# Third mixture of a decoder kernel: eight blocks of rows made on chip by products with slot tables

## The reference

```python
x_flat = x.reshape(s * b, h)                       # 1024 x 128
probs = jax.nn.softmax(x_flat @ gate_w.T / TEMPERATURE, axis=-1)
topk_probs, topk_idx = jax.lax.top_k(probs, TOPK)  # TOPK = 2
hidden = jax.nn.relu(jnp.einsum('th,ehf->tef', x_flat, w1) + b1[None])   # f = 512
all_out = jnp.einsum('tef,efh->teh', hidden, w2) + b2[None]
gathered = jnp.take_along_axis(all_out, topk_idx[:, :, None], axis=1)
y_flat = jnp.sum(gathered * topk_probs[:, :, None], axis=1)
```

## Time and profile before

| | us |
|---|---|
| median of 3 runs | 1390.26 (1382.43 to 1390.34) |
| the profiled execution, whole time | 1389.44 |
| its span, from the first to the last instruction | 1387.6 |
| PE busy | 1152.1 |
| DVE busy | 889.7 |
| POOL busy | 272.7 |

### The profile page before, as it was taken

How to read it: one execution, slowest core, us unless ns; L and a number is a source line. 1 busy time by engine, 2 the same in 40 slices (tenths; PEclk the granted TensorE clock), 3 DMA queues, 4 the chain that set the end, 5 groups by cost and what they waited for, 6 DMA issues and landing times.

```text
span 1387.6 us, 26416 instructions
## 1 busy us (share of the span) xinstructions
PE 1152.1 (83%) x9412; PEld 712.4 (51%) x9412; DVE 889.7 (64%) x2335; ACT 711.6 (51%) x1456; POOL 272.7 (20%) x558
## 2 busy tenths in 40 slices
PE   4878997894887499668999999999944968989994
PEld 2333333892343498455666666666634833333332
DVE  5758985445667354877766666677740176777866
ACT  3665883231733123325666665776712535646674
POOL 2522221461010274100000000000024404212220
PEclk9798998996897699889999999999976978989998
DMA  7421248554311496200000000011034734211200
GB/s 179 104 73 42 67 129 344 196 174 144 79 52 61 160 309 216 97 0 1 1 1 1 1 1 1 9 46 47 24 110 133 263 121 103 64 48 48 54 8 16
DMA packets 91362, 122.45 MB, mean 88 GB/s; under 512 B 11073, under 2 KB 69134, under 8 KB 90254
## 3 DMA queue, kind: packets, MB, share of 16 engines
q1 hardware_dynamic: 87010, 112.11, 26.1%
q0 software_dynamic: 4224, 8.66, 1.9%
HBM read 89.73 MB, written 30.02 MB: 86 GB/s over the span
## 4 chain that ended last, share of the span: by engine, by line
PE 64%; DVE 14%; DMA 6%; issue 5%; ACT 5%; POOL 3%; SPq 3%; DVEq 0%; ACTq 0%; POOLq 0%
PE ps L2717 7%; PE ps L2724 7%; PE ps L1170 6%; PE ps L2732 6%; PE ps L1865 4%; PE ps L920 4%; PE ps L1878 3%; PE ps L929 3%; PE ps L2806 2%; PE ps L1867 2%; PE ps L2813 2%; PE ps L1082 2%; PE ps L1205 2%; POOL scr_x L2120 2%; PE ps L970 2%
## 5 line engine op out<-in xcount | busy, mean ns | idle before, releaser
L1170 PE MATMUL ps<-probs,vaug 128*32 128x256 f32 (+1 forms) x1792 | 144.9, 398 | 12.0 <-ACT probs L1134 7.5
L2924 DVE CUSTOM_DVE_ANT_0 wring<-ps,probs 128x768 f32<-128x768 f32 x128 | 122.5, 957 | 46.2 <-PE ps L2717 45.6
L2883 ACT COPY qs<-ps 128x768 f32<-128x768 f32 x128 | 102.3, 800 | 90.3 <-PE ps L2724 90.3
L1125 ACT ACTIVATE probs<-ps 128x512 f32<-128x512 f32 x192 | 104.2, 595 | 64.3 <-PE ps L970 64.1
L273 POOL TENSOR_TENSOR rstd<-veps,mhalf 128x4 f32<-128x4 f32 (+2 forms) x28 | 26.5, 948 | 538.2 <-DVE veps L241 503.0
L1002 DVE TENSOR_REDUCE mx<-ps 128x2 f32<-128x1024 f32 (+1 forms) x96 | 115.5, 1220 | 20.7 <-PE ps L920 19.9
L1129 ACT ACTIVATE probs<-ps 128x512 f32<-128x512 f32 x192 | 104.8, 595 | 40.9 <-PE ps L1082 39.8
L2864 ACT ACTIVATE wring<-wring,r 128x768 f32<-128x768 f32 x128 | 120.8, 944 | 3.9 <-DVE r L2927 3.9
L2724 PE MATMUL ps<-ident,wring 128*128 128x128 f32 x768 | 110.2, 280 | 3.2 <-DVE wring L2968 3.2
L2724 PEld LDWEIGHTS ps<-ident,wring 128*128 128x128 f32 x768 | 83.4, 140 | 41.9 <-issue 35.3
L2717 PE MATMUL ps<-probs 64*128 64x512 f32 (+1 forms) x512 | 100.5, 511 | 1.1 <-DVE r L2924 1.1
(11 more groups left out here) (383 smaller groups left out, 2405.3 us busy)
## 6 DMA issues: line engine op xcount, KB each, us to landing
wring<-in_L_ffn_w SPq DMA_DIRECT2D x21, 768.0 KB, 5.9
wring<-in_L_ffn_w SPq DMA_DIRECT2D x19, 514.0 KB, 4.9
ks<-in_L_ffn_w SPq DMA_DIRECT2D x8, 768.0 KB, 16.5
qs<-in_L_ffn_w SPq DMA_DIRECT2D x6, 768.0 KB, 11.3
probs<-scr_x SPq DMA_DIRECT2D x14, 256.0 KB, 4.0
qs<-scr_q SPq DMA_DIRECT2D x18, 192.0 KB
qs<-scr_qx SPq DMA_DIRECT2D x16, 192.0 KB
probs<-in_L_ffn_w SPq DMA_DIRECT2D x4, 768.0 KB
```

Of the source, the lines that this page charges most:

```text
L1125: act.activation(probs[:, s % 2, 2 * c + r, kt0 * S:(kt0 + 2) * S], bank(self.banks(3, k)[r]), ACT.Exp).then_inc(p_exp.sem, 1)
L1170: ins = pe.matmul(ps[32 * j:32 * j + 32, self.av_bank(s), q0:S], vaug[:, s % 2, kt, j, :], probs[:, s % 2, j, at:at + S - q0], start=(kt = ...
L2883: act.copy(self.pT[:, g % 2, j, :, k * P:(k + 1) * P], self.buffer("turn", i, 0, KV).rearrange("p (t n) -> p t n", n=P)).then_inc(self.out ...
L2924: dve.tensor_tensor_reduce(self.sc[:, s, :], src, self.maskb[:, u // (2 * PR), :], 1.0, -3.0e38, ALU.add, ALU.max, self.top[:, s:s + 1]).t ...
```

## The change

- Rows of blocks 0 to 7 (groups 0 and 1) are made on chip. For each group g and token tile t DVE makes a slot table of 128 x 512 (`hot_vector`): at row p, column j a one where either slot of token p is column j of the group. It takes two instructions, a comparison of the column numbers (`self.numbers`, in `gated`) with the first slot, and a second comparison added to it. PE multiplies `h[:, t, :]` with the table and sums over the eight tiles in one bank (`permute_tensor`), which gives the group's rows already turned; ACT copies them to `xbT` as before. There are 16 tables in a ring of four, in the memory of `v`. Twelve are made behind the slots in `place_vector`, the last four behind the results of blocks 0 and 1. PE does the first eight products before block 0 and two more before each of blocks 1 to 4.
- The 16 scatters stay. The loads of groups 0 and 1 go, and group g + 2 is loaded behind the weights of block 4g + 3. The wait for all 16 scatters stays behind the weights of block 3.
- The map and the shares move behind the products: DVE does them in pieces at blocks 4 to 8 and PE behind the up matmuls of block 7. The column sums of the last part's weights (`weights_vector`) move from block 6 to block 10.
- `constant_rows` moves from ahead of SP's loop to behind the weights of block 12.

```diff
@@ -1577,13 +1577,13 @@
     r_exp = counter("r_exp", [1] * 3)
     sorted_out = counter("sorted_out", [NT, 0, 2 * NT], 16)
     h_spill = counter("h_spill", [pair_loads[8], 4, 0], 16)
-    hot = counter("hot", [m["choices"] for m in MOES])
+    hot = counter("hot", [1, 2, 2 * NT + 2])
     map_mm = counter("map_mm", [1] * 3)
     mapped = counter("mapped", [2] * 3)
-    x_in = [counter(f"x_in{i}", [len(range(i, groups[0], 2)), 2, len(range(i, groups[2], 2))], 16) for i in range(2)]
+    x_in = [counter(f"x_in{i}", [len(range(i, groups[0], 2)), 2, len(range(i, groups[2], 2)) - 1], 16) for i in range(2)]
     x_rows = [counter(f"x_rows{i}", [0, sum(min(2, blocks[1] - 2 * g) for g in range(i, groups[1], 4)), 0],
                       16) for i in range(4)]
-    x_tp = counter("x_tp", groups)
+    x_tp = counter("x_tp", [groups[0], groups[1], groups[2] - 2])
...
@@ -1704,7 +1708,8 @@
             m, n = self.m, self.group(g)
             rows = slice(g * self.gb * P, (g * self.gb + n) * P)
             if g >= self.held:
-                sp.wait_ge(x_tp.sem, x_tp.at(m, g - self.held + 1))
+                if g - self.held >= self.turned_in:
+                    sp.wait_ge(x_tp.sem, x_tp.at(m, g - self.held - self.turned_in + 1))
...
@@ -1726,8 +1731,6 @@
                     for k in range(2):
                         sp.dma_start(scr_h[1 + k * T:1 + (k + 1) * T, :].rearrange("(t p) d -> p t d", p=P)[:, at, :],
                                      h[:, at, :]).then_inc(h_spill.sem, 16)
-            if self.relu:
-                constant_rows(sp)
...
@@ -1741,9 +1744,10 @@
                 if self.sorted:
                     if b == self.early:
                         sp.wait_ge(sorted_out.sem, sorted_out.at(m, self.choices * NT))
-                        self.x_sync(sp, 0)
-                    if b == self.early or b > self.early and b % self.gb == 0 and b // self.gb + 1 < self.ng:
-                        self.x_sync(sp, b // self.gb + 1)
+                    if b % self.gb == self.early and b // self.gb + self.turned_in < self.ng:
+                        self.x_sync(sp, b // self.gb + self.turned_in)
+                    if b == 12:
+                        constant_rows(sp)
...
+            if not self.turned_in:
+                self.map_tensor(pe)
+            for b in range(self.nb):
+                g = b // self.gb
+                if b == 0 and self.turned_in:
+                    self.permute_tensor(pe, range(NT))
+                elif b == 0:
+                    self.turn_tensor(pe, 0)
+                if b % self.gb == self.gb // 2 and g + 1 < self.ng and g + 1 >= self.turned_in:
+                    self.turn_tensor(pe, g + 1)
+                if 0 < b <= self.gb and self.turned_in:
+                    self.permute_tensor(pe, range(NT + 2 * b - 2, NT + 2 * b))
+                self.up_tensor(pe, b)
+                if b:
+                    self.down_tensor(pe, b - 1)
+                if self.turned_in and b == 7:
+                    self.map_tensor(pe)
...
+        def permute_tensor(self, pe, steps):
+
+            m = self.m
+            for i in steps:
+                g, t = divmod(i, NT)
+                pe.wait_ge(hot.sem, hot.at(m, i + 1))
+                ins = pe.matmul(bank(6 + g % 2), h[:, t, :], self.slot_hot[:, i % 4, :], start=(t == 0), stop=(t == NT - 1))
+                ins.then_inc(perm_mm.sem, 1)
+
+        def hot_vector(self, dve, i):
+
+            m = self.m
+            g, t = divmod(i, NT)
+            out, slot = self.slot_hot[:, i % 4, :], slotf[:, g, :, t:t + 1]
+            if i >= 4:
+                dve.wait_ge(perm_mm.sem, perm_mm.at(m, i - 3))
+            link(dve, dchain, dve.tensor_scalar(out, self.numbers, slot[:, 0, :], None, ALU.is_equal))
+            dve.scalar_tensor_tensor(out=out, in0=self.numbers, scalar=slot[:, 1, :], in1=out, op0=ALU.is_equal,
+                                     op1=ALU.add).then_inc(hot.sem, 1)
+
+        def numbers_vector(self, dve):
+
+            for k in range(4):
+                ins = dve.tensor_scalar(self.numbers[:, k * P:(k + 1) * P], down[:, 34:162], float(k * P), None, ALU.add)
+            link(dve, dchain, ins)
 
...
@@ -1881,7 +1927,10 @@
 
         def turn_scalar(self, act, g):
             m, n, first = self.m, self.group(g), self.at(g * self.gb)
-            act.wait_ge(x_tp.sem, x_tp.at(m, g + 1))
+            if g < self.turned_in:
+                act.wait_ge(perm_mm.sem, perm_mm.at(m, (g + 1) * NT))
+            else:
+                act.wait_ge(x_tp.sem, x_tp.at(m, g - self.turned_in + 1))
...
@@ -1908,7 +1957,9 @@
                 k, g = self.sh + b, b // self.gb
                 if b == 0:
                     self.turn_scalar(act, 0)
-                if b % self.gb == self.gb // 2 and g + 1 < self.ng:
+                if self.turned_in and b == self.gb:
+                    self.turn_scalar(act, 1)
+                if b % self.gb == self.gb // 2 and g + 1 < self.ng and (g or not self.turned_in):
                     self.turn_scalar(act, g + 1)
...
@@ -2002,10 +2053,18 @@
             if self.sorted:
                 dve.tensor_scalar(place[:, 0:self.choices * NT], slotf[:, 0, 0:self.choices, :].rearrange("p k t -> p (k t)"),
                                   -1.0, None, ALU.add).then_inc(placed.sem, 1)
-            if self.choices == 2:
+            if self.turned_in:
+                link(dve, dchain, dve.tensor_scalar(slotf[:, 1, :, :], slotf[:, 0, :, :], -512.0, None, ALU.add))
+                for i in range(NT + 4):
+                    self.hot_vector(dve, i)
+            elif self.choices == 2:
                 self.map_vector(dve)
-            if self.choices == 2:
-
+                self.shares_vector(dve)
+
...
@@ -2083,12 +2163,23 @@
                     if y >= RING:
                         dve.wait_ge(y_spill[y % 4].sem, y_spill[y % 4].at(m, y // 4))
                     dve.tensor_copy(yblk[:, self.at(y), :], bank(4 + y % 2, 0, P)).then_inc(y_sb.sem, 1)
+                if self.turned_in and b in (1, 2):
+                    self.hot_vector(dve, NT + 2 + 2 * b)
+                    self.hot_vector(dve, NT + 3 + 2 * b)
+                if self.turned_in and b == 4:
+                    self.map_rows_vector(dve)
+                if self.turned_in and b in (5, 6):
+                    self.map_hot_vector(dve, b - 5)
+                if self.turned_in and b == 7:
+                    self.map_found_vector(dve)
+                if self.turned_in and b == 8:
+                    self.shares_vector(dve)
                 if m == 1 and 2 <= b < 2 + 2 * CTX_STEPS:
                     others[7].context_vector(dve, *divmod(b - 2, CTX_STEPS))
-                if m == 2 and b == 6:
+                if m == 2 and b == 10:
                     others[11].weights_vector(dve)
```

More of the change, by code:

```diff
@@ L1629, in __init__ @@
             self.gb, self.held = GB[m], RING // GB[m]
+            self.turned_in = 2 if self.relu else 0
+            self.hots = self.turned_in * NT
             at = 4608 if self.shared else 5632
             hots = tmp[:, at:at + 512 * self.choices].bitcast(BF16)
+            self.slot_hot = v[:, :, :].rearrange("p (i k) d -> p i (k d)", k=4)
+            self.numbers = gated[:, 0, :]
             self.row_hot = hots.rearrange("p (i j) -> p i j", j=P)
@@ L1790, in tensor, with map_tensor @@
                 self.shared_down_tensor(pe)
+            if not self.turned_in:
[15 more added lines that the diff above has]
+                    self.map_tensor(pe)
+            self.down_tensor(pe, self.nb - 1)
+            if self.relu:
+                pe.wait_ge(y_sb.sem, y_sb.at(m, self.nb))
+                for t in range(NT):
+                    ins = pe.transpose(bank(0 + t // 4, t % 4 * P, t % 4 * P + P)[0:8, :], comb[:, t, 0:8], ident[:, :])
+                ins.then_inc(perm_mm.sem, 1)
+                pe.wait_ge(combT_sb.sem, combT_sb.at(m, 1))
+                for t in range(NT):
+                    ins = pe.matmul(bank(2 + t // 4, t % 4 * P, t % 4 * P + P), combT[:, t * P:(t + 1) * P],
+                                    b2r[:, :], start=True, stop=True)
+                ins.then_inc(perm_mm.sem, 1)
+        def map_tensor(self, pe):
+            m = self.m
+            if self.turned_in:
+                pe.wait_ge(x_T.sem, x_T.at(m, self.turned_in))
             for k in range(self.choices):
-                pe.wait_ge(hot.sem, hot.at(m, k + 1))
+                pe.wait_ge(hot.sem, hot.at(m, self.hots + k + 1))
                 for i in range(k * NT, (k + 1) * NT):
@@ L1850, in turn_tensor @@
                 pe.wait_ge(x_T.sem, x_T.at(m, g))
+            if self.turned_in and g == 3:
+                pe.wait_ge(mapped.sem, mapped.at(m, 1))
             for k in range(n):
@@ L2024, in map_vector, with map_slots, map_rows_vector @@
         def map_vector(self, dve):
-            m, n = self.m, self.choices * NT
+            self.map_rows_vector(dve)
+            for k in range(self.choices):
```

(22 more changed lines are left out.)

36 lines of the change are left out of this document (12 added, 24 removed).

## The result

The changed kernel takes 1394.66 us (median of 10 runs, 1390.83 to 1398.01); the kernel before, on the same chip in the same rounds, 1387.88 (1382.43 to 1392.05). The ratio is 1.0045, 95% interval 1.0025 to 1.0065: 6.8 us slower. That is within 1% and inside the range, but the forecast was 1.4 us faster, so its direction is wrong. The profiled execution took 1392.43, span 1390.6, 3.0 more than before's; the stage that the change touches, read from slots to last copy, accounts for 4.8 more, less 1.5 for slots that are ready earlier (1029.78 against 1031.29). Those profiles are one execution each, and the two are closer together than the medians are.

What follows compares the result with a forecast made beforehand. The prediction took the kernel as mostly bound by PE (83% busy). Block 4 at 1062.8 plus 45.0 us put the last copy at 1107.8 instead of 1109.2, 1.4 us earlier: forecast 1388, range 1377 to 1397.

Steps and rivals of the forecast that it cites:

- What bounds the kernel: Whole kernel: mostly bound by PE, busy 83% of the span; PE stands still around the third mixture's 16 scatters.
- part 1: Products up to block 4: block 0 starts at about 1043 instead of 1059.1, a gain of 16 us on the page.
- Part 2: Block 4's weights, still behind the scatters: block 4 starts at 1060.0 against 1067.81, so 8 of 16 us are left.
- Part 3: Scatters beside DVE's tables: each waits for the DVE instruction in progress, the last lands 2.8 us later; block 4 at 1062.8.
- Part 4: From block 4 to the last copy: 45.0 us instead of 41.4, from several small terms.
- The constant rows: Term from block 4 on: four issues ahead of block 13's weights and 288 KB in a full queue, 1.2 us.
- Results wait for the map: Term from block 4 on: result scatters start only behind the map, block 8's copy waits for the fifth; 0.8 us.
- The clock: Term from block 4 on: PE, after standing still, may begin block 4 at clock 0.50; 1.5 us, between 0 and 2.7.
- A: Rival: scatters aren't slowed and small terms hide behind each other, stage ends 7 us earlier, 1382; chance 0.28.
- The lock: Rival B: DVE's tables hold the scatters' port longer, 6 us in all, stage ends 7 us later, 1396; chance 0.13.
- C: Rival: the whole 16 us of the products come out, needing block 4's weights by 1056; 1373; chance 0.05.
- L: Theory added after the measurement, not in the prediction: from block 4 on the weight loads' own rate sets the pace.

Runs made afterwards that it cites:

- e9: Kernel before, with eight useless DVE instructions of 1.25 us added beside the scatters, four with two inputs, then four with one; 1392.85 us in one execution.
- e2: Kernel before, with only the constant rows moved behind the weights of block 12; 1400.16 us, ratio 1.0100 to before.
- e11: Changed kernel with the map at block 4 instead of block 7, constant rows still late; 1396.05 us, ratio 1.0044 to before.
- e12: e1 with the map at block 4 instead of block 7; 1381.96 us, ratio 0.9956 to before.
- e8: e1 plus four loads, together 288 KB over 128 partitions, behind the weights of block 12; 1388.59 us, ratio 0.9995 to before.
- e1: Changed kernel with the constant rows back ahead of SP's loop; 1389.48 us, ratio 1.0010 to before.
- e5: e1 with block 4's weights issued ahead of the wait for the scatters, some row loads one block later; 1386.16 us, ratio 0.9984 to before.
- e6: e5 with the map at block 4 instead of block 7; 1377.52 us, ratio 0.9922 to before.
- e3: Changed kernel with the late constant rows sent one to a transfer, ten transfers instead of four, each written as 16 runs; 1397.85 us, ratio 1.0077 to before.

## Why the prediction was wrong, step by step

**What bounds the kernel, and part 1: right.** Block 0 started 11.8 us after the slots (11.7 forecast), PE would have been ready for block 4 when ACT's second copy ended, at 1055.00 + 0.59 = 1055.59, that is 25.8 us after the slots (24.7 forecast), and this was hidden, as said, by the wait for block 4's weights.

**Part 2: right, term by term.** From the last landing (1052.77) to the issue 1.17 us (1.25 forecast), landing 4.45 (4.4), a wait of 3.46 us on PE (4). Block 4 started 28.65 us after the slots, where the same steps without a slowed scatter give 28.7.

**Part 3: wrong, and in the kernel's favour.** The step "one has to stand still until the DVE instruction in progress ends ... 2.8 us" didn't occur: the 16 scatters' starts spread over 20.0 us, 20.1 in before. That DVE can hold a scatter is so (e9), but two rows didn't say which of DVE's instructions do, and I took the two engines' instructions to meet at random. They fell into step: in the second view of after each scatter starts 0.04 or 0.05 us behind the start of a two-input instruction, and the pair of DVE's instructions grew by some 0.08 us, from 0.48 + 0.75 to 0.54 + 0.77, until a table took as long as a scatter's period, 1.26. The tables paid, by nearly nothing, and the scatters as a whole nothing.

**Part 4: here the direction was lost.** 54.1 us instead of 45.0, in two of its terms.

- "The constant rows ... 1.2, between 0 and 2.4." The term was worked out from bytes at the mean rate of the queue. Measured: 5.2 us in the changed kernel, 12.0 in the kernel before (e2), 14.1 with the map early (e11 against e12). What failed is the choice of the row: bytes at a mean rate price a transfer like e8's, of short runs over all partitions (it cost nothing), and not one of a few long rows into a few partitions. Before, the rows ran in a quiet time: in the stretches there, from 1022 to 1031, the queues moved no more than 95 GB/s at a share of 0.43. These stretches stand in no row above, and alone they wouldn't have told the reason, since little else was moved then.
- "Results wait for the map ... 0.8, between 0 and 3." The mechanism was right, the copy of block 8 waiting for the scatter of block 4's results; the size was wrong. In e1, without the rows, PE stood still for 5.49 us against the 2 to 3 that I took:

```profile
1070.51 0.18 DVE L2131 TENSOR_TENSOR probs<-probs 128x23 int32<-128x23 int32 x1
...
1072.15 1.06 PE L1924 MATMUL ps<-wring,probs 128*128 128x128 f32 x8
...
1081.82 2.05 PE L1924 MATMUL ps<-wring,probs 128*128 128x128 f32 x8 [5.49 <-DVE probs L2165]
```

The map is there at 1070.69. The fifth scatter lands at 1076.49 + 4.77 = 1081.26, 10.6 us behind it, where I had 7.3: its landing takes 4.77 in a full queue instead of the 2.2 of a quiet one. And the copy of block 8 is due at 1073.21, 2.5 us behind the map, where I had 4 to 5. I also let the stall hide behind a wait for weights, which it doesn't. The late map is worth 7.5 us (e1 against e12).

"The clock ... 1.5" was for a start of block 4 at 0.50. In the changed kernel it didn't come: those eight up matmuls took 1.16 us and the next group 1.06, at a granted clock of 1.00. In e1 they did start low (2.08 us). The fall that the changed kernel had came behind the stall, with 2.04 us for the next down matmuls; it is part of what both terms measured. The map's 16 matmuls took 0.56 us (0.6 forecast); the weights in hand (-0.5) are too small for these runs to hold against anything.

**The rivals.** A (1382) was right on the scatters and wrong on "the small terms hide behind each other". The lock (1396) met the time within 2 us by a mechanism that didn't occur. It had also taken the map's wait at its upper end, 3; a time that fits is no evidence for its reasons. C needed block 4's weights earlier: e5 made exactly that, with the rows ahead, and won only 3.3 us over e1; the copy's stall was still there. With the map early too (e6) the kernel reaches 1377.52.

**Still open:** how the row transfers slow the others. That their place in the queue costs this much is shown (e1, e2, e11 against e12), and that it isn't their bytes (e8). Whether it is the few partitions, the packets of 32 KB or where they are read from isn't: e3 was to tell and left the packets whole. Rows over 128 partitions in long packets, or short packets into the same eight partitions, would tell. L was only argued.

## What to carry to other kernels

Price a transfer by its shape as well as by its bytes: a few long rows into a few partitions belong in a quiet time, for here the load behind them landed after 15.3 to 16.4 us instead of 3.4 to 6.4, and the view to look for is few GB/s beside a DMA share near 1 (or, one row to a transfer, beside a low one). When results are held back until something is ready, work out the backlog from the landing time in a full queue, and look at which buffer's wait it will meet. When two stalls may lie over each other, undo them one by one and both together: here neither of the two repairs predicts what they give together. And look at whether an edit did what it was made for: the packet counts of e3's page tell that it didn't.

## What the runs showed of the hardware that I had not expected

- 288 KB in eight rows of 32 KB and two of 16, into eight partitions, raised a weight load from 3.4 to 6.4 us to 16.12 (e2) and a scatter's landing from 4.77 (e1) to 12.02, with 99 to 127 GB/s at a share of 0.76 to 1.00 in the changed kernel. As many bytes over 128 partitions, in runs of 1 KB and less, were free (1388.59 against 1389.48).
- Writing a row of 32 KB as 16 runs of 2 KB didn't make smaller packets: the page's count stayed at 85954.
- DVE instructions of 0.54 and 0.77 us beside indirect transfers fell into step with them and cost the 16 of them nothing (20.0 us against 20.1); four of 1.25 us with two inputs stretched one transfer from 0.96 to 1.34 us, and four of 1.25 us with one input stretched three, to as much as 2.22.
- A scatter of 128 rows lands in 2.2 us in a quiet queue and took 4.77 in a full one (e1).
